# Four layers of attention and feed-forward on one core: last attention, projection and normalisation merged into one block, queries loaded in token halves, shared expert summed unit by unit

## The reference

```python
# fourth attention: 16 heads of 16, keys and values from ctx, all 1024 tokens attend to all 1024
q = fq_sym((ln(x) @ Wq + bq) / 4, per head row)       # rounded to 127 steps
k = fq_sym(ctx @ Wk + bk); v = fq_sym(ctx @ Wv + bv, over tokens)
p = fq_unsigned(softmax(q @ k.T))                     # rounded to 255 steps
x = x + (p @ v) @ Wp + bp
# fourth feed-forward: 8 experts, 2 chosen for each token, and a shared one
h = ln(x)
top, e = top_k(h @ router_w, 2); s = softmax(top)
routed = sum_k s[k] * ((silu(h @ w1g[e_k]) * (h @ w1u[e_k])) @ w2[e_k])   # 512 hidden
shared = (silu(h @ w_gate) * (h @ w_up)) @ w_down                          # 1024 hidden
x = x + routed + shared
```

## Time and profile before

| | |
|---|---|
| Median of 3 runs | 1105.83 us (1105.2 to 1108.23) |
| Profiled execution, own time | 1113.83 us |
| Its span, first to last instruction | 1112.1 us |
| Mean granted clock of PE | 0.865 of full |
| PE busy | 919.5 us (83%) |
| DVE / ACT / POOL busy | 620.2 / 526.3 / 252.4 us |
| Fourth attention, first maximum to last exponential | 648.3 to 832.4 us |
| Last head, scaling, projection, normalisation | 832.4 to 859.6 us |
| Fourth feed-forward | 859.9 to 1112.1 us |

### The profile page before, as it was taken

One profiled execution on the slowest core, in us unless ns is written; L12 is line 12 of the kernel. 1 busy time (PEld: TensorE's weight loads), 2 busy tenths in 40 slices (PEclk: granted clock), 3 DMA queues, 4 the chain that ended last, 5 costly groups with the idle time before them and its releaser, 6 DMA issues. The chain is left out here.

```text
span 1112.1 us, 15443 instructions
## 1 busy us (share of the span) xinstructions
PE 919.5 (83%) x5390; PEld 539.1 (48%) x5416; DVE 620.2 (56%) x1304; ACT 526.3 (47%) x794; POOL 252.4 (23%) x297
## 2 busy tenths in 40 slices
PE   5698987998998548799799467787866978999996
PEld 2244435666487324444357423333435454666654
DVE  4577755445345875745456579999985411111123
ACT  3166664222423665578643169898982102222210
POOL 4010100000000001313542127667771230000031
PEclk9599999899899869999899765655567899999999
DMA  3613301000357004667144547878650021111022
GB/s 123 155 35 74 110 15 47 1 1 1 127 65 80 0 1 121 184 162 129 44 189 83 196 86 150 162 150 185 108 91 13 24 71 29 41 45 48 24 59 70
DMA packets 130445, 91.64 MB, mean 82 GB/s; under 512 B 92805, under 2 KB 119631, under 8 KB 128591
## 3 DMA queue, kind: packets, MB, share of 16 engines
q1 hardware_dynamic: 125522, 83.45, 33.4%
q0 software_dynamic: 1536, 4.20, 1.2%
q10 hardware_dynamic: 3312, 3.02, 0.8%
HBM read 56.09 MB, written 15.86 MB: 65 GB/s over the span
## 5 line engine op out<-in xcount | busy, mean ns | idle before, releaser
L2270 ACT ACTIVATE sb_l_E<-PS,sb_l_NB,sb_L3SQS 128x1024 uint8<-128x1024 f32 x128 | 154.4, 1207 | 22.7 <-DVE sb_l_NB L2304 13.0
L2301 DVE TENSOR_REDUCE sb_l_NM<-PS 128x1 f32<-128x1024 f32 x128 | 155.5, 1215 | 5.3 <-PE PS L2244 5.3
L2244 PE MATMUL PS<-sb_l_K,sb_l_Q 128*128 128x512 bf16 x232 | 115.4, 589 | 40.9 <-ACT sb_l_E L2270 33.1
L2209 POOL CAST sb_l_ET<-sb_l_EP 128x1024 bf16<-128x1024 uint8 x128 | 128.5, 1040 | 79.0 <-DMA sb_l_EP<-sb_l_E 77.3
L613 DVE TENSOR_REDUCE sb_negmax<-PS 128x2 f32<-128x512 f32 x128 | 84.1, 690 | 31.6 <-PE PS L463 31.4
L2254 PEld LDWEIGHTS PS<-sb_L3VI,sb_l_ET 128*128 128x128 bf16 x1024 | 54.8, 112 | 72.5 <-issue 46.8
L1368 PE MATMUL PS<-sb_L3w,sb_block_xT 128*128 x184 | 83.0, 594 | 4.5 <-DVE sb_hidden L1458 3.0
L599 ACT ACTIVATE sb_E<-PS 128x1024 f32<-128x1024 f32 x64 | 65.4, 1023 | 42.2 <-PE PS L526 42.2
L923 ACT ACTIVATE sb_E<-PS 128x1024 f32<-128x1024 f32 x64 | 65.3, 1024 | 24.6 <-PE PS L830 20.9
L463 PE MATMUL PS<-sb_K,sb_Q 96*128 96x256 bf16 x256 | 53.9, 302 | 15.9 <-ACT sb_negmax_T L573 10.3
L1458 DVE TENSOR_TENSOR sb_hidden<-sb_hidden,PS 128x512 f32<-128x512 f32 x23 | 15.8, 688 | 88.2 <-ACT sb_hidden L1423 88.2
(11 more groups left out here) (336 smaller groups left out, 1720.9 us busy)
## 6 DMA issues: line engine op xcount, KB each, us to landing
sb_Q<-q SPq DMA_DIRECT2D x48, 192.0 KB
sb_L3w<-L3w SPq DMA_DIRECT2D x16, 512.0 KB, 6.7
sb_K<-k SPq DMA_DIRECT2D x24, 192.0 KB
sb_W2E<-L3w SPq DMA_DIRECT2D x8, 512.0 KB, 4.7
q<-sb_q_parts SPq DMA_DIRECT2D x12, 256.0 KB, 4.0
xs<-zero_row SPq DMA_DIRECT2D x1, 2944.0 KB, 47.9
sb_block_x<-xs SPq DMA_DIRECT2D x23, 128.0 KB, 2.2
ys<-sb_block_y ACTq DMA_DIRECT2D x23, 128.0 KB, 2.4
```

The source lines that it names most:

```text
L2209: return eng.tensor_copy(ET[:, u % CRING], EP[:, u // 2 % TRING, :, :, u % 2])
L2244: ins = pe.matmul(core.bank(2 * (n % SRING) + half), Q[:, h % RING, t * P:(t + 1) * P], K[:, h % RING, half * HALF:(half + 1) * HALF], sta ...
L2270: act.activation(E[:, n // 2 % ERING, :, n % 2], S(n), ACT.Exp, bias=NB[:, n:n + 1], scale=scale_of(h, t), accum_out=ZS[:, n:n + 1]).then_ ...
L2301: dve.tensor_reduce(NM[:, n:n + 1], S(n), axis=AX.X, op=ALU.max, negate=True).then_inc(maxed, 1)
```

## The change

1. `attention_l3` now also holds the scaling of the weights, the projection and the normalisation. The weights are scaled by DVE before the first unit, the bias is loaded at the start and added to X by POOL after the queries are rounded. When the mixing of unit 121 has been issued PE turns features 0 to 127 of the attention output (`turn_out(0)`, heads 0 to 7) into banks 4 and 5; ACT copies them after its last exponential; PE multiplies tiles 0 to 3 by the first half of the weights after mixing unit 123 and tiles 4 to 7 after mixing unit 125. Only features 128 to 255 are turned and multiplied after the last head.
2. The cast of the last unit, 127, is done by DVE and no longer by POOL.
3. `load_q` copies half of the tokens: for the first four heads 12 DMAs for tokens 0 to 511 as soon as ACT has copied the first half, then 12 more for tokens 512 to 1023, on the one semaphore `q_late`, for which PE waits at unit 4. The warming matmuls and the load of the exponential table move to the first half. PE waits for the other copies at unit 2.
4. In `moe_silu` each shared unit is multiplied by its chunk of the down weights right after the next unit's first matmuls (`shared_part`), the four tiles accumulating side by side in two banks over eight units; DVE adds two tiles at once (`add_shared`), for tokens 512 to 1023 after all merges. `HS` shrinks to two buffers. Blocks are turned two ahead, and the first two straight after the last shared unit of the first half. The scatter begins when the first of the two slot lists is ready.

```diff
 attention_l3
-    by_pool = [True for u in range(NU)]
+    by_pool = [u != NU - 1 for u in range(NU)]
-                def load_q(h):
+                def load_q(h, tokens, done):
                     for i in range(PARTS):
-                        sp.dma_start(Q[HD * i:HD * (i + 1), h % RING, :], QT[HD * (h % 8):HD * (h % 8 + 1), h // 8, :]
-                                     ).then_inc(q_in[h % RING], 16)
+                        sp.dma_start(Q[HD * i:HD * (i + 1), h % RING, tokens],
+                                     QT[HD * (h % 8):HD * (h % 8 + 1), h // 8, tokens]).then_inc(done, 16)
+                sp.dma_start(BB[:, :], bias_dram.partition_broadcast(P)).then_inc(loaded, 16)
...
+                sp.wait_ge(out_a, 1)
+                for h in range(RING):
+                    load_q(h, slice(0, HALF), q_in[h])
                 sp.wait_ge(out_a, 2)
                 for h in range(RING):
-                    load_q(h)
+                    load_q(h, slice(HALF, TOK), q_late)
...
+                pool.wait_ge(loaded, 16)
+                pool.wait_ge(q_whole, 2)
+                for t in range(NT):
+                    pool.tensor_tensor(core.X[:, t, :], core.X[:, t, :], BB[:, :], ALU.add).then_inc(x_biased, 1)
...
+                def turn_out(c):
+                    for half in range(2):
+                        for j in range(HN):
+                            ins = pe.transpose(core.PS[:, OUT_FIRST + half, j * P:(j + 1) * P],
+                                               core.XN[:, HN * half + j, c * P:(c + 1) * P], core.identf[:, :])
+                        ins.then_inc(out_turned, 1)
+                def project_out(c, half):
+                    for t in range(HN * half, HN * half + HN):
+                        ins = pe.matmul(core.PS[:, t // 2, (t % 2) * D:(t % 2 + 1) * D],
+                                        core.XT[:, c, t * P:(t + 1) * P], Wo[:, c, :],
+                                        start=(c == 0 and t % 2 == 0), stop=(c == NC - 1 and t % 2 == 1))
+                        if c == NC - 1 and t % 2:
+                            ins.then_inc(out_done, 1)
...
-                pe.wait_ge(out_a, 2)
-                pe.wait_ge(out_v, 2)
-                for i in range(WARM):
+                    for i in range(WARM if half == 0 else 0):
...
+                        if h == 0 and t == NT // 2:
+                            pe.wait_ge(q_late, 16 * PARTS * RING)
+                        if n == 2:
+                            pe.wait_ge(out_a, 2)
+                            pe.wait_ge(out_v, 2)
...
+                        if u == NU - 7:
+                            pe.wait_ge(exped, NU - 2)
+                            turn_out(0)
+                        if u == NU - 5:
+                            pe.wait_ge(xt_a, 2)
+                            pe.wait_ge(exped, NU)
+                            pe.wait_ge(rows_scaled, NC)
+                            project_out(0, 0)
+                        if u == NU - 3:
+                            project_out(0, 1)
+                pe.wait_ge(normed, HEADS)
+                turn_out(1)
+                pe.wait_ge(xt_a, 3)
+                project_out(1, 0)
+                pe.wait_ge(xt_v, 1)
+                project_out(1, 1)
...
+                dve.wait_ge(x_biased, NT)
+                add_out(0)
+                add_out(1)
+                stats(0)
+                stats(1)
+                mean_var(0)
+                add_out(2)
+                normalise(0)
+                add_out(3)
+                stats(2)
+                stats(3)
+                mean_var(1)
+                normalise(1)
 layers_kernel
-            scale_rows(core, w["L3Wp"], SV)
-        out_project(core, w["L3Wp"], dram["L3bp"])
-        core.recycle()
-        layer_norm(core, [])
 moe_silu
-            pool.wait_ge(routed, 1)
-            for t in range(NT):
-                for k in range(2):
+            for k in range(2):
+                pool.wait_ge(placed, k + 1)
+                for t in range(NT):
...
+            def shared_part(n):
+                kind, half, k = units[n]
+                pe.wait_ge(hidden, n + 1)
+                if half and k == 0:
+                    pe.wait_ge(h_out, BLOCKS)
+                    pe.wait_ge(x_out, BLOCKS)
+                for t in range(4):
+                    ins = pe.matmul(core.PS[:, SHARED_BANKS[half][t // 2], t % 2 * D:(t % 2 + 1) * D],
+                                    HS[:, k % 2, t * P:(t + 1) * P], WD[:, k, :], start=(k == 0 and t % 2 == 0), stop=(k == SC - 1 and t % 2 == 1))
+                    ins.then_inc(shared_down, 1)
...
-            for n in range(NU + 2):
+            for n in range(NU + 1):
                 if n < NU:
                     go_up(n)
                 if n == 1:
                     pe_counts(pe)
+                if n >= 1 and units[n - 1][0] == "shared" and n != SC:
+                    shared_part(n - 1)
+                if n == SC - 1:
+                    shared_part(n)
+                    turn_x(0)
+                    turn_x(1)
...
+                if n < NU and units[n][0] == "block" and units[n][2] + 2 < BLOCKS:
+                    turn_x(units[n][2] + 2)
...
+            def add_shared(half, pair):
+                dve.wait_ge(shared_down, 4 * SC * (half + 1) - 2 + 2 * pair)
+                X = core.X[:, 4 * half + 2 * pair:4 * half + 2 * pair + 2, :].rearrange("p t d -> p (t d)")
+                if half:
+                    dve.wait_ge(merged, 2 * NT)
+                dve.tensor_tensor(X, X, core.bank(SHARED_BANKS[half][pair]), ALU.add).then_inc(x_added, 1)
...
+                if n == NU - 2:
+                    dve.wait_ge(x_added, 2)
                     for t in range(4):
                         merge(t)
+                if n == NU - 1:
+                    for t in range(4, NT):
+                        merge(t)
+            for pair in range(2):
+                add_shared(1, pair)
```

More of the change, by code:

```diff
@@ L1149, in route @@
         "logits", "vmax", "diff", "ex", "masked", "counted", "drawn", "made", "routed"))
+    placed = core.sem("placed")
     G = [core.sb(ctx, f"gate{k}", [P, NT], F32) for k in range(2)]
@@ L1276, in moe_silu @@
     block_unit = lambda b: SC + b
[L1277 to L1284, removed]
+    shared_index = lambda n: n if n < SC else n - BLOCKS
+    SHARED_BANKS = ((6, 7), (6, 4))
     XRING, YRING = 4, 3
@@ L1378, in turn_hidden, with go_down @@
                 ins.then_inc(h_turned, 1)
[L1380 to L1387, removed]
-                else:
[L1389 to L1392, removed]
-                ins.then_inc(down, 1)
+            def go_down(b):
+                if b == 0:
+                    pe.wait_ge(x_added, 2)
+                else:
+                    pe.wait_ge(y_out, b)
+                pe.wait_ge(h_out, b + 1)
+                for k in range(HC):
+                    w = core.W2E[:, bass.ds(expert[b], 1), k * D:(k + 1) * D].rearrange("p e n -> p (e n)")
+                    ins = pe.matmul(core.PS[:, 7, 0:D], HT[:, b % 2, k, :], w, start=(k == 0), stop=(k == HC - 1))
+                ins.then_inc(down, 1)
+            def shared_part(n):
[8 more added lines that the diff above has]
+                    ins.then_inc(shared_down, 1)
             pe_logits(pe)
-            for n in range(NU + 2):
+            for n in range(NU + 1):
                 if n < NU:
@@ L1460, in _ @@
+            dve_choose(dve)
+            for n in range(NU):
+                dve.wait_ge(silued, n + 1)
+                dve.tensor_tensor(hidden_of(n), hidden_of(n), core.bank(2 * (n % 2) + 1), ALU.mult
+                                  ).then_inc(hidden, 1)
                 if n == 1:
                     dve_place(dve)
-                for kind, i in downs_at[n]:
-                    dve.wait_ge(down, down_count[(kind, i)])
-                    if kind == "block":
-                        if i >= YRING:
-                            dve.wait_ge(y_stored[i % YRING], 16 * (i // YRING))
-                        dve.tensor_copy(YB[:, i % YRING, :], core.PS[:, 7, 0:D]).then_inc(y_out, 1)
-                    else:
-                        dve.tensor_tensor(core.X[:, i, :], core.X[:, i, :], core.PS[:, 7, 0:D], ALU.add
-                                          ).then_inc(y_out, 1)
-                        dve.wait_ge(y_out, down_count[(kind, i)])
-                        if i >= 4:
-                            merge(i)
@@ L1474, in _ @@
-                if n == NU - SC + 7:
+                if n == SC - 1:
+                    for pair in range(2):
+                        add_shared(0, pair)
+                if n >= 2 and units[n - 2][0] == "block":
+                    b = units[n - 2][2]
+                    dve.wait_ge(down, b + 1)
+                    if b >= YRING:
+                        dve.wait_ge(y_stored[b % YRING], 16 * (b // YRING))
+                    dve.tensor_copy(YB[:, b % YRING, :], core.PS[:, 7, 0:D]).then_inc(y_out, 1)
```

158 lines of the change are left out of this document (112 added, 46 removed).

## The result

The changed kernel takes 1095.76 us (median of 4 runs, 1095.04 to 1096.54) against 1105.86 (4 runs, 1105.2 to 1108.23): ratio 0.9896 [0.9878, 0.9913], 10.1 us less. The forecast was 25.1 less, range 1074.5 to 1089. The direction was right and the size was not. Yet the profiled executions differ by 1113.83 - 1096.42 = 17.4 us, and from the normalisation ahead of the attention to the end of the span by 491.2 - 467.0 = 24.2. So two things have to be found: where 7 us went between that stage difference and the whole, and where another 7 went between the profiles and the medians. The profiled execution of before (1113.83) is none of its four timed runs; the one of the changed kernel (1096.42) is one of its four.

The account below looks back on a forecast made before the run. DVE and ACT pace the attention, dependency chains its start and end, PE the steady feed-forward blocks, with waits around them. Terms 0.7 - 5.4 - 10.2 - 3.5 - 6.7 = -25.1 us, from 1105.83 to 1080.7; range 1074.5 to 1089.

Parts of the forecast that it names:

- Queries in halves: Attention start: 24 query issues at 0.63 us each make unit 4 wait, losing 0.7 us.
- issues get cheaper with the bytes: Rival, attention start: half-size query copies cost less to issue, start gains 4.5 us, total 1075.5 us; chance 0.11.
- Last head, projection, normalisation: Attention end: three borders, bias adds and half the projection leave the chain, last mixing 2.3 later; gain 5.4 us.
- Shared sums, first half: Feed-forward before block 0: PE multiplies shared chunks without waiting, block 0 at 910.7 against 920.95; gain 10.2 us.
- Blocks turned two ahead: First feed-forward blocks: 7.7 us replace 11.22 from first to third block; gain 3.5 us.
- The end: Feed-forward tail: shared chunks hidden behind merges, span ends at 1105.4 instead of 1112.1; gain 6.7 us.
- that execution lies 8.0 above the median of the runs; I take the difference over unchanged: Final sum: the profile's 25.1 us gain was applied unchanged to the median 1105.83, giving 1080.7.
- the 3 us stall comes back at the tail: Rival, feed-forward tail: DVE's unexplained shared-add wait recurs, end 3.2 us later, total 1083.9 us; chance 0.14.
- Held up: Rival: early projection delays the last heads and first blocks stay loose, sum -20.3, total 1085.5 us; chance 0.12.
- the granted clock: Rival, feed-forward: each block at half clock costs 5.8 us more, eight such give 1127 us; chance 0.03.

Follow-up runs that it names:

- warm_router: Changed kernel plus 7 + 9 idle matmuls in PE's gaps of the last normalisation, to keep the clock up for the router: 1095.6 us, 0.9898 to before.
- split_head0: Changed kernel with only head 0's queries copied in halves, heads 1 to 3 whole: 1089.2 us, 0.9816 to before.
- moe_only: Kernel before with only the changed feed-forward (`route` and `moe_silu`): 1098.2 us, 0.9841 to before.
- attn_only: Kernel before with only the changed attention, projection and normalisation: 1115.6 us, 0.9999 to before.
- before_no_moves: Kernel before without POOL's 16 indirect scatters and 16 gathers: 1109.1 us, 1.0005 to before.
- after_no_moves: Changed kernel without POOL's indirect scatters and gathers: 1094.1 us, 0.9873 to before.
- after_again: Changed kernel, unaltered, profiled and timed a second time: 1097.3 us, 0.9842 to before.
- after_look: Changed kernel, unaltered, profiled once more as a single execution: 1100.2 us.
- before_no_gather: Kernel before without POOL's 16 gathers and the merge's wait, scatters kept: 1112.3 us, 0.996 to before.
- best: Changed kernel with only head 0's queries in halves, 7 + 9 idle matmuls in the last normalisation, and `project_out(0, 1)` behind mixing 127: 1088.1 us, 0.9825 to before.
- split_warm: Changed kernel with only head 0's queries in halves and 7 + 9 idle matmuls in the last normalisation: 1089.2 us, 0.9741 to before.

## Why the prediction was right in its parts and wrong in its number

**Queries in halves, +0.7.** Measured +1.0 (18.12 - 17.15), up to 1.6 against other profiles of before (16.53 to 17.16); the issues at their full price. Right; "issues get cheaper with the bytes" falls.

**Last head, projection, normalisation, -5.4.** Measured 30.24 - 24.27 = -6.0. The last mixing came 9.91 us after the last maximum against 8.79, 1.1 later where 2.3 was forecast; the rest took 14.05 where 13.4 was. With the same last heads it came 9.91 to 11.18 after in the other profiles, and 8.41 in the three with head 0 alone in halves, by where PE's clock rose: four to eight us after the last maximum it was granted 0.64 in the changed kernel, 0.50 in warm_router (11.14) and 1.00 in split_head0 (8.41). Right in the stage, and DVE's cast is worth nothing, as said; but the router behind it lost 1.4 to 2.2 us of it again (c 52.26 to 53.08 against 50.83 in moe_only), and no pair of medians shows a gain of the attention's part (attn_only 0.9999).

**Shared sums, first half, -10.2.** In the profiles -8.7, and -3.8 against before_no_moves, without the late add. In moe_only block 0 starts 50.83 us after the router, the 50.8 forecast; beside the new attention it is 52.26, since the router is at half clock (6.97 against 5.0). That cost was in no term. Of the 8.7, 4.9 us is the late wake-up and the clock after it.

**Blocks turned two ahead, -3.5.** By the starts in the timeline 11.2 before and 7.8 after: -3.4. Right.

**The end, -6.7.** Measured 57.9 - 51.3 = -6.6, of which 4.9 is the late wake-up: without the gathers the kernel before takes 53.0. The number was met because the profile it was taken from had the wait; without it the term is -1.7.

**The step that failed** is the last of the sum, "that execution lies 8.0 above the median of the runs; I take the difference over unchanged". The 24.2 us measured between the two stage sums is within 1 us of the 25.1 forecast. But 9.2 of it are late wake-ups that the profiled execution had, and that stood in the terms for the shared sums and the end. At the median, 1105.83, they cannot all be there: 1105.83 less 1.7 outside the span less 491.2 leaves 612.9 us for the stages ahead, where all 20 profiles show 620.1 to 629.7; with 482.0 it leaves 622.1. So the work itself gains 482.0 - 467.0 = 15.0 us, as the medians of before_no_moves and after_no_moves differ, and 1105.8 - 15.0 = 1090.8 would have been the forecast. (One microsecond of the 15.0 is scatter in the query stage ahead of ACT's copy.) That the runs of the result were free of late wake-ups is worked out from spans, not seen in a trace. The remaining 5 us to 1095.76 lie, by the same reckoning, in the stages ahead: 622.1 for before, and 627.66 in the changed profile. Their scatter shows in both kernels, and what makes it is open.

The rival "the 3 us stall comes back at the tail" was right on some chips, at another engine (after_again, after_look: d 54.2 and 54.8 against 51.3), but it was priced against a kernel that had it too. The text priced one stall at 3.2 us and called it a doubt about the new kernel; it should have asked whether the runs of the old one had it. "Held up" and "the granted clock" don't show: steady blocks still take 5.8.

## What to carry to other kernels

A profiled execution well above the median is not an offset to carry over: look for waits in it that no record explains, price the kernel with and without them, and count as gain only what the median can hold. Splitting transfers pays only as long as the issues ahead of the consumers don't grow: against whole copies one head in halves gained 2.5 us, four heads lost 2.9. Work moved ahead of a chain of f32 matmuls is worth more than its length if it brings the clock up for what follows: here 7.4 us for eight turns, two copies and eight matmuls (16 records) of 3.7 us at full clock. A gain in one stage can be lost in the next: behind the new end of the attention the router ran at half clock.

## What the runs showed of the hardware

- In the profiles from three of the chips a wake-up of DVE or ACT by PE comes late, 0.9 to 2.9 us after the last of a series of indirect DMAs has been issued, and in those from two others none does; leaving the gathers out takes the one of the tail away and leaves the other (before_no_gather).
- The same PE group takes 3.72 us, also after 2.1 or 2.2 us of idle time, and 5.2 to 5.4 after 3.2 to 3.8.
- Unchanged stages of 620 us differ by up to 9.6 us between executions at a mean granted clock of 0.856 to 0.872.
- Eight f32 records of 256 columns take 1.97 us in the changed kernel and 3.71 in best, by the clock at their place; two placements of the same early projection differ by 2.5 us in the end of the attention (24.52 in best, 22.05 in split_warm).
